# Attention features: stacked operands by DMA copies, and the Newton steps of the inverse norms on GpSimd

## What is computed

```python
qkv = x @ Wqkv + bqkv                        # 16 heads of 16 dimensions
xn = x / max(norm(x), 1e-12)                 # for q and for k, each head by itself
proj = einsum('bhtd,rhdm->rbhtm', xn, omega) # 2 x 32 features a head
arg = clip(proj * sqrt(2s) - s, -20, 20)
feat = exp(arg) / sqrt(32) * sqrt(weight)
# then in chunks of 128 tokens: causal (qf kf^T) v, plus qf times the state, over the normaliser
```

## Time and profile before

| | |
|---|---|
| median of the runs | 1459.89 us |
| profiled execution, its time | 1448.13 us |
| its span, first to last instruction | 1446.5 us |
| TensorE matmul busy, over the span | 1371.3 us (95%) |
| VectorE busy | 914.3 us (63%) |
| ScalarE busy | 684.4 us (47%) |
| GpSimd busy | 551.6 us (38%) |
| mean granted TensorE clock | 0.976 |

### The profile page before, as it was taken

How to read it: one execution, slowest core, us unless ns; L and a number is a source line. 1 busy time by engine, 2 the same in 40 slices (tenths; PEclk the granted TensorE clock), 3 DMA queues, 4 the chain that set the end, 5 groups by cost and what they waited for, 6 DMA issues and landing times. The chain is left out here.

```text
span 1446.5 us, 33923 instructions
## 1 busy us (share of the span) xinstructions
PE 1371.3 (95%) x12256; PEld 1190.8 (82%) x12256; DVE 914.3 (63%) x1944; ACT 684.4 (47%) x1257; POOL 551.6 (38%) x503
## 2 busy tenths in 40 slices
PE   6989999989999999999998999999999999999994
PEld 5778888877677777777777988888899999999984
DVE  4666767676776877877774464444555555555547
ACT  2356667544545455445444433223355555555533
POOL 0144555442254354454310006422344444444421
PEclk9799999998999999999999999999999999999997
DMA  6333333105133133233115204633788888888885
GB/s 223 128 136 123 111 133 128 52 15 181 45 100 120 57 117 123 65 131 102 45 60 219 104 30 162 263 111 122 188 227 233 234 233 234 233 234 234 248 258 213
DMA packets 103869, 216.12 MB, mean 149 GB/s; under 512 B 18544, under 2 KB 74224, under 8 KB 96624
## 3 DMA queue, kind: packets, MB, share of 16 engines
q1 hardware_dynamic: 79552, 159.87, 33.8%
q0 software_dynamic: 23088, 54.31, 13.1%
q10 hardware_dynamic: 1152, 0.93, 0.2%
HBM read 150.23 MB, written 64.84 MB: 149 GB/s over the span
## 5 line engine op out<-in xcount | busy, mean ns | idle before, releaser
L2637 PE MATMUL ps<-e_xhl,s_whl 128*128 128x256 f32 x1848 | 245.7, 282 | 0.0
L2637 PEld LDWEIGHTS ps<-e_xhl,s_whl 128*128 128x128 f32 x1848 | 231.0, 189 | 0.2 <-issue 0.2
L2019 PE MATMUL ps<-s_xhl,s_whl 128*128 128x512 f32 x660 | 164.5, 398 | 1.4 <-PEq L1108 1.4
L2468 POOL DMA_INDIRECT xs<-e_y,e_slot_id x78 | 122.1, 1566 | 90.5 <-ACT e_y L2502 71.4
L492 POOL TENSOR_TENSOR b_hhl<-b_h,b_hhl 128x512 fp32r<-128x512 f32 x64 | 94.7, 1482 | 139.7 <-ACT b_hhl L756 118.3
L2019 PEld LDWEIGHTS ps<-s_xhl,s_whl 128*128 128x128 f32 x660 | 122.1, 190 | 26.5 <-issue 1.8
L2616 PE MATMUL ps<-s_whl,e_ghl 128*128 128x256 f32 x936 | 139.3, 285 | 0.6 <-issue 0.6
L2716 DVE TENSOR_TENSOR e_g<-ps,e_act_h 128x256 f32<-128x256 f32 x156 | 66.2, 424 | 112.8 <-ACT e_act_h L2515 112.8
L2616 PEld LDWEIGHTS ps<-s_whl,e_ghl 128*128 128x128 f32 x936 | 121.8, 189 | 0.8 <-issue 0.7
L589 PE MATMUL ps<-b_w,b_hhl 128*128 128x256 f32 x768 | 105.3, 287 | 6.3 <-DVE b_turned_rows L862 5.6
L2515 ACT ACTIVATE e_act_h<-ps 128x256 f32<-128x256 f32 x156 | 60.1, 385 | 107.9 <-PE ps L2637 102.4
(11 more groups left out here) (384 smaller groups left out, 2737.2 us busy)
## 6 DMA issues: line engine op xcount, KB each, us to landing
s_whl<-wlo SPq DMA_DIRECT2D x38, 1024.0 KB, 5.0
s_whl<-wlo SPq DMA_DIRECT2D x38, 512.0 KB, 3.7
c_eraw<-in_expert_w POOLq DMA_DIRECT2D x24, 512.0 KB, 4.9
wlo<-c_elo POOLq DMA_DIRECT2D x24, 512.0 KB, 3.0
wall<-in_expert_w SPq DMA_DIRECT2D x8, 1536.0 KB, 9.2
xg<-b_zeros POOLq DMA_DIRECT2D x13, 780.0 KB, 3.9
e_xr<-xg SPq DMA_DIRECT2D x39, 260.0 KB, 3.8
x<-rows_out SPq DMA_DIRECT2D x16, 512.0 KB, 3.2
```

Source lines behind the costliest of these rows:

```text
L2019: mm = pe.matmul(ps[:, H + 2 * (m % 2) + w, :], whl[:, wp, e, lo:lo + P], xhl[:, k, xp, kd, :], start=q == 0, stop=q == 3 * KD - 1)
L2468: gp.indirect_dma_start(xs, bass.IndirectOffsetOnAxis(ap=slot_id[:, i, b:b + 1], axis=0), y[:, k, b, :], None, compute_op=ALU.add).then_in ...
L2637: mm = pe.matmul(ps[:, H + m, w * SLOT:(w + 1) * SLOT], whl[:, k, wp, lo:lo + P], xhl[:, k, xp, kd, :], start=q == 0, stop=q == 3 * KD - 1)
```

## The change

Part one: the features of a pair are done in two matmuls of 512 columns, one for queries and one for keys, on 96 rows. The right operand is stacked: 32 rows of high parts, again the same 32 rows of high parts, and 32 rows of low parts; the left operand has omega's high, low and high parts in the same rows. The read-out of FN goes to a buffer `stage`, which heads 0 to 7 and heads 8 to 15 use in turn, and SyncE copies from it to the stacked buffers `fs`: three DMAs of 32 rows by 4 KB for each pair, so 12 after FN 2 and 12 after FN 3 of each chunk. For the first chunk the first 12 are issued at the end of the mixer's SyncE list. `features` waits for the three copies of its pair, and ScalarE's read-out of FN 0 and FN 1 waits for the four pairs that still read the stage.

Part two: the three Newton steps are done by GpSimd, four instructions each, each waiting for the one before. VectorE keeps the sums, the guess, and one multiplication more.

Part three, the order: FT 1, FQ 0 to 3, BO 3, BW, BO 0, BO 1, FN 0 and FN 2 move in the table. FN 0 and FN 2 move from turn 7 (A and B) to turn 6 (B and C). The sums move to turn 4. The third piece of expert weights on GpSimd goes behind the squares. SyncE stores the output of a chunk one body later, and four of the six loads of shared weights are issued at the end of its list, since the stacked buffers lie in their place. The loads of two chunks for the next phase move from body 6 to body 7.

```diff
+QUAD = PAIRS // KD
+STACK = 3 * MF
...
+def stack_pair(sp, ahead, t):
+
+    g = t % QUAD
+    for n, part in enumerate((0, 0, 1)):
+        sp.dma_start(ahead.fs[t // QUAD][n * MF:(n + 1) * MF, g].bitcast(F32), ahead.stage[g * MF:(g + 1) * MF, part].bitcast(F32)).then_inc(ahead.stacked[t], 16)
...
+                if is_(i, STEPS + 1):
+                    sp.wait_ge(s["fn_lo"], 2)
+                    for t in range(QUAD):
+                        stack_pair(sp, ahead, t)
...
-                      2: ((A_, "FT", 0), (B_, "FT", 1), (C_, "BO", 3)),
-                      3: ((A_, "FQ", 0), (B_, "FQ", 1), (C_, "BC", 1)),
-                      4: ((A_, "FQ", 2), (B_, "FQ", 3), (C_, "BW", 0)),
-                      5: ((A_, "BW", 1), (C_, "BO", 0)),
-                      6: ((A_, "BO", 1),),
-                      7: ((A_, "FN", 0), (B_, "FN", 2))}
+                      2: ((A_, "FT", 0), (A_, "FT", 1), (B_, "BO", 3), (C_, "FQ", 0)),
+                      3: ((A_, "FQ", 1), (B_, "FQ", 2), (C_, "FQ", 3), (C_, "BC", 1)),
+                      4: ((B_, "BW", 0),),
+                      5: ((A_, "BW", 1),),
+                      6: ((A_, "BO", 0), (B_, "FN", 0), (C_, "FN", 2)),
+                      7: ((C_, "BO", 1),)}
...
-            for n in range(NCH):
+
+            def load_shared(n):
                 sp.dma_start(ahead.raw[:, n * CC:(n + 1) * CC], swf[:, n * CC:(n + 1) * CC]).then_inc(ahead.raw_in[n], 16)
 
+            for n in range(2):
+                load_shared(n)
+
+            def stack(i, half):
+                k1 = (i, "FN", 3) if half else (i - 1, "FN", 2)
+                sp.wait_ge(s["x_free"], x_index(*k1) + 1)
+                for t in range(QUAD * half, QUAD * (half + 1)):
+                    if not isinstance(i, int) or i > 0:
+                        sp.wait_ge(s["feat_done"], 2 * (PAIRS * (i - 1) + t + 1))
+                    stack_pair(sp, ahead, t)
...
+                if last_rows(i):
+                    sp.wait_ge(s["feat_done"], 2 * PAIRS_ALL)
+                    for n in range(2, NCH):
+                        load_shared(n)
...
+            def norm_roots(i):
+                ch = Chain(gp, s["norm_root"], 4 * 3)
+                ch.turn(i)
+                gp.wait_ge(s["guessed"], i + 1)
+                gp.wait_ge(s["norm_own"], 5 * (i + 1))
+                nv, nr, nt = (nrm[:, k, :] for k in range(3))
+                for n in range(3):
+                    ch.link(gp.tensor_tensor(nt, nr, nr, ALU.mult))
+                    ch.link(gp.tensor_tensor(nt, nt, nv, ALU.mult))
+                    ch.link(gp.tensor_tensor(nt, nt, three_halves[:, 0:1].to_broadcast([P, BATCH * 2 * HEADS1]), ALU.add))
+                    ch.link(gp.tensor_tensor(nr, nt, nr, ALU.mult))
+                ch.end()
...
-                rows = [slice(2 * HD * at, 2 * HD * (at + 1)) for at in (t % 4, (t + 1) % 4)]
-                for c, (lp, rp) in enumerate(PARTS):
-                    for q in range(2):
-                        mm = pe.matmul(ps[:, FB + q, :], om[rows[q], lp, t, :], qkt[rows[q], rp, KD * q + t // 4, :],
-                                       start=c == 0, stop=c == 2)
-                        if c == 2:
-                            mm.then_inc(s["feat_done"], 1)
+                for q in range(2):
+                    pe.matmul(ps[:, FB + q, :], om[0:STACK, t, :], fs[t // QUAD][0:STACK, t % QUAD, q, :],
+                              start=True, stop=True).then_inc(s["feat_done"], 1)
...
+                        if name == "FN" and a < KD:
+                            for before in range(QUAD * (1 - a), QUAD * (2 - a)):
+                                act.wait_ge(stacked[before], STACKED * (i + 1))
```

More of the change, by code:

```diff
@@ L194, in __init__ @@
         self.x_in = [sem(f"x_in{k}") for k in range(2)]
+        self.stacked = [sem(f"stacked{t}") for t in range(PAIRS)]
         self.raw_hi, self.raw_lo, self.turned, self.xhi_ready, self.xlo_ready, self.h_done = (
@@ L1251, in body @@
                     sp.dma_start(xr[:], x2[i + 2]).then_inc(s["x_in"], 16)
+                if is_step(i - 2):
+                    sp.wait_ge(s["out_ready"], PRIMED + i - 1)
+                    sp.dma_start(x3[i - 2], out[:]).then_inc(s["stored"], 16)
                 if is_step(i - 1) and (not isinstance(i, int) or i < STEPS):
@@ L1254, in body @@
                     sp.dma_start(xb[:], x2[i]).then_inc(s["res_in"], 16)
-                if is_step(i - 1) and not last_rows(i):
-                    sp.wait_ge(s["out_ready"], PRIMED + i)
-                    sp.dma_start(x3[i - 1], out[:]).then_inc(s["stored"], 16)
-                if isinstance(i, int) and i == LAST - 1:
+                if is_step(i + 1):
+                    stack(i + 1, 0)
+                if isinstance(i, int) and i == LAST:
+                    for t in range(QUAD, PAIRS):
+                        sp.wait_ge(stacked[t], STACKED * STEPS)
                     sp.wait_ge(s["stored"], PRIMED + 16 * 2)
@@ L1266, in _ @@
             sp.wait_ge(x2_stored, PRIMED + 16 * STEPS)
-            with sp.Fori(1, LAST - 1) as i:
+            body(1)
+            with sp.Fori(2, LAST - 1) as i:
                 body(i)
@@ L1308, in body @@
                         gp.tensor_tensor(sq[:, bb], qk[:, bb], qk[:, bb], ALU.mult).then_inc(s["sq_ready"], 1)
-                    by_chunk = lambda ap: ap.rearrange("p (m c h) d -> p m c h d", c=KD, h=HEADS1 // KD)
+                if not isinstance(i, int) or 1 <= i < LAST:
+                    split_expert_weights(i, range(2, EPER - 1))
+                if is_step(i + 1):
+                    norm_roots(i)
                     for c in range(KD):
-                        gp.wait_ge(s["rnorm_ready"], f)
                         heads = lambda ap: ap.rearrange("p b (s c h d) -> p (b s) c h d", s=2, c=KD, d=HD)[:, :, c]
@@ L1664, in _ @@
             nv, nr, nt = nrm[:, 0, :], nrm[:, 1, :], nrm[:, 2, :]
[L1665 removed]
+            NORM_OWN = 2 + 3
             def squares(ch, f, half):
@@ L1740, in body @@
                     x_evac(i, t, A_)
-                    if front and t == 5:
-                        squares(norm, i + 1, 1)
-                        norm_guess(norm)
-                        norm_newton(norm, False)
+                    if front and t == 4:
+                        squares(norm, i + 1, 0)
                     if isinstance(i, int) and i == 0 and t == 1:
@@ L1757, in body @@
                     if front and t == 4:
-                        squares(norm, i + 1, 0)
+                        squares(norm, i + 1, 1)
+                        norm_guess(norm)
                     if isinstance(i, int) and i == 0:
@@ L2864 @@
     omega_in = np.asarray(L1_attn_omega)
-    omega = np.zeros((P, PAIRS, P), omega_in.dtype)
-    per = P // HD
+    pairs = np.zeros((MF, PAIRS, P), omega_in.dtype)
     for h in range(HEADS1):
-        r0, c0 = HD * (h % per), FD * (h % 2)
-        omega[r0:r0 + HD, h // 2, c0:c0 + FD] = omega_in[:, h].transpose(1, 0, 2).reshape(HD, FD)
-        r0 = (r0 + 2 * HD) % P
-        omega[r0:r0 + HD, h // 2, c0:c0 + FD] = omega_in[:, h].transpose(1, 0, 2).reshape(HD, FD)
-    def keys_moved(w):
-        w = np.asarray(w).copy()
-        for lo in (D, D + P):
-            w[..., lo:lo + P] = np.roll(w[..., lo:lo + P], 2 * HD, axis=-1)
-        return w
+        r0, c0 = HD * (h % 2), FD * (h % 2)
+        pairs[r0:r0 + HD, h // 2, c0:c0 + FD] = omega_in[:, h].transpose(1, 0, 2).reshape(HD, FD)
+    omega = np.tile(pairs, (P // MF, 1, 1))
     def per_feature(v):
```

68 lines of the change are left out of this document (32 added, 36 removed).

## The result

The changed kernel takes 1517.9 us (median of 4 runs, 1515.7 to 1520.2), the kernel before on the same chip 1460.7. The ratio is 1.0388, 95% interval 1.0363 to 1.0413: 57 us slower. The forecast of 1470.6 had the sign right and the size wrong; the range ended at 1490.

The account below looks back on a forecast made before the run. TensorE's list was taken to bound the attention (412.4 of 428.0 us busy). Gains of 21.8 and 13 against costs of 16.8, 3.5, 14, 5, 4.7 and 1.5 gave +10.7 us: 1470.6 us, range 1440 to 1490.

Parts of the forecast that it names:

- The features: TensorE's feature matmuls: two on 96 rows take 0.55 us instead of 0.89, gaining 21.8 us over 64 pairs.
- All on the path: Claim that the whole 21.8 us saved on TensorE's feature matmuls shortens the kernel.
- The old waits: TensorE's 15.6 us idle in the attention: 13 taken as gone, with a gain between 0 and 13.
- The roots on GpSimd: Newton steps on GpSimd: TensorE waits 2.4 us at FN 0 in seven bodies, costing 16.8 us.
- The copies: SyncE's copies to the stacked buffers: 3.5 us of waits at pair 0 and 14 us at BC 0.
- more than 2 us: Sign of being wrong: pair 0's features wait for the copies by more than this.
- the copies set the pace: Rival: copies land late at half rate or beside GpSimd's 1 MB, BC 0 waits 3.6 us; 1487 us, chance 0.20.
- The clock: TensorE's granted clock falls after waits of 2.4 us in seven bodies: 5 us lost, between 0 and 14.
- The two ends: Attention starts 4.7 us later behind 12 copy issues; four late shared-weight loads cost 1.5 us at the end.
- Nothing: Claim that the new order of FT, FQ, BO and BW and some smaller moves cost no time.

Follow-up runs that it names:

- b_table: Kernel before with only the new order: changed step table, Newton steps on VectorE in turn 5, six feature matmuls, no copies; 1465.8 us, ratio 1.0032.
- a_small_copies: Changed kernel with as many copies in the attention's loop, each 16 KB instead of 128 KB, so the result differs; 1490.7 us, ratio 1.0312.
- b_fn_early: Kernel before with FN 2 moved ahead of the context in turn 7; 1436.0 us beside 1445.7, ratio 0.9934.
- a_fill: Changed kernel with unused matmuls in TensorE's two longest idle stretches, ten ahead of FN 0 and sixteen ahead of pair 0; 1499.0 us, ratio 1.0354.

## Why the prediction was right or wrong

**The features.** A pair's two matmuls take about 0.57 us at full clock up to what follows (610.69 to 611.26, say), as worked out. "All on the path" failed: 14 us came in the run alone, not 21.8, because VectorE's mask is late next (15.3 us).

**The old waits.** 13 of 15.6 taken as gone: the two rows went, but with the new order came 7.0 us of BO 3's wait for FT's read-out (4.7 in b_table), and behind the copies 5.4 of BO 2's. As a gain this term was nearly nothing.

**The roots on GpSimd.** 0.41 and a step of 0.07 were forecast; measured 0.40 and 0.46, with 0.08 between two. FN 0 was to wait 2.4 us, 16.8 in all; it waited 2.7 to 3.8, 20.2 in all. This is the step that was right. What the whole move costs, 10 us, is less than its waits, as the mask holds TensorE otherwise. (The prediction's upper bound counts 0.60 us without the step between two; with it the wait would be 4.7 us and not 4.)

**The copies.** This is the step that failed. It took 0.39 us an issue from the earlier trace rows, a DRAM transfer; the median is 0.59 for a copy, thick or thin. It took a landing of 2.3, and the median is 2.4, but the longest is 10.0: beside GpSimd's 1 MB pair 0 starts 6.7 us after the first issue (634.79 - 628.12), and the last copy lands 10.9 after it (639.01 - 628.12, where ScalarE reads out FN 1), not 6.6 (11 x 0.39 + 2.3). With the 1.5 us of read-outs, which came as forecast, that is 12.4 us after FN 2 and not 8.1. Pair 0's wait was put at 0.5 us, "between 0 and 1.2"; it was 0.4 to 4.6, 2.6 in the mean, and "more than 2 us" was the prediction's own sign of being wrong. The chain behind the twelfth copy was named rightly as far as ScalarE at FN 1. Its consumer was not: the first to want a bank back is BO 2 in turn 0, behind FN 1, and not BC 0 in turn 1 behind FN 3. It was priced at 14 us with 3.5 for pair 0; the copies, with what they do to the clock, cost 38. The rival "the copies set the pace", 1487 us, had the mechanism and the point from which it decides (the twelfth copy later than 10 us); it had a chance of 0.20 and was itself short.

**The clock.** 5 us forecast, "between 0 and 14". It does fall in every body behind FN 0 and behind late copies. Filling both idle stretches brought the steady bodies' clock from 0.92 to 0.97 and gave 6.3 us in the attention, none of them in the steady bodies. So the term had the right order of size, and what is lost beyond it is mostly the copies' chain.

**The two ends.** The start was forecast at 4.7 us, from the issue of 0.39; it cost 7.2 (332.79 instead of 325.60). The end was forecast at 1.5:

```profile
819.15 2.46 SPq L1266 DMA_DIRECT2D s_raw<-in_shared_w  x4
...
822.21 4.30 PE L2067 MATMUL ps<-s_xhl,s_whl 128*128 128x512 f32 x12 [2.59 <-PEq L1127]
...
823.69 6.28 SPq L1921 DMA_DIRECT2D wall<-x  x5
829.91 1.37 PE L2036 MATMUL ps<-wall,d_xts 128*128 128x8 f32 x8 [3.41 <-DMA d_ones<-in_masks]
```

The four loads are issued in 2.46 us as said, but the masks behind them land late ("6 if the constants land late" was the bound): five issues that took 3.15 us in the earlier trace rows take 6.28, TensorE waits 3.41 for the masks instead of 0.9, and the clock falls with it. On chip 9, without the gap, the rest after the attention is 678.0 and 679.4 us in the changed kernel's variants and 668.2 and 670.1 in those of before: some 9 us. In the first 100 us of it the granted clock is 0.94 in a_small_copies and 0.98 in b_fn_early. No run puts the loads back to the front, so that they are the cause of all 9 us isn't shown.

**"Nothing" for the new order** was wrong by 4 to 6 us (b_table; 442.6 against 437.0).

The sum against the measured 57 us in the forecast's terms: features and old waits together -12 instead of -35, roots +10 instead of +17, order +5 instead of 0, copies with their clock +38 instead of +22, ends +16 instead of +6. Of the 46 us between the sums, 23 are gains that the helpers withheld, 16 the copies, 10 the ends and 5 the order, less 7 for the roots.

## What to carry to other kernels

When a helper stands in a chain between two pieces of the bound engine's list, its idle time isn't slack: only the distance from its input to its consumer counts. Price a series of DMAs by the moment the last one lands beside whatever else moves then, and ask who waits for the last to free its source; the first consumer's wait can vanish without the kernel getting faster. And work taken from an engine that is 96% busy is still not worth its full time when the next helper is only a microsecond ahead; here the move of one step, FN 2, made the kernel 10 us faster, and the whole change made it 57 us slower.

## What the runs showed of the hardware

- While only copies from SBUF to SBUF on 32 rows ran, the DMA engines showed as full (share 0.90 to 1.01) at 201 to 223 GB/s; with other transfers beside them the same engines moved 328.
- An issue of such a copy takes 0.59 us on SyncE for 16 KB as for 128 KB, against 0.39 in the earlier trace rows; on GpSimd's queue 0.49.
- GpSimd needs 0.40 or 0.46 us for 128 elements a partition, by the line, in the same chain; it needed 0.20 for 4.
- Idle time of 2.77 us on TensorE was followed by 3 us and more at a granted clock of 0.50; with ten matmuls laid into it (a_fill, 618 to 624 us) the clock stayed at 1.00.
- The kernel before took 1445.7 us on one chip and 1461 on the others; the "remote" gap in the shared experts, which most of the profiled executions show, was in none of the four on that chip.
